# A fused attention and feed-forward layer on one core: the order of each attention turn, and the passage to the feed-forward part

## What is computed

```python
x = x + tanh(g_xattn) * attention_part(layernorm(x), ctx)
x = x + tanh(g_ffn) * ffn_part(layernorm(x))

# attention_part: the first 257 context rows only, so all 128 here
q = rms_norm(x @ q_w.T + q_b) * norm_q_w         # 16 heads of 32
k = rms_norm(ctx @ k_img_w.T + k_img_b) * norm_k_img_w
v = ctx @ v_img_w.T + v_img_b
out = softmax(q k^T / sqrt(32)) v @ o_w.T + o_b

# ffn_part
route = top_k(h @ gate_w, 2)[0].sum(-1)           # h: [tokens, 512]
y = square(relu(h @ up_w)) @ down_w + (h @ expert_weight) * route
y = layernorm(y) * ln_gamma + ln_beta             # up_w: 512 x 2048
```

## Time and profile before

| | |
|---|---|
| Median of 3 runs | 1451.87 us (1451.42 to 1457.24) |
| Profiled execution, its own time | 1454.03 us |
| Its span, first to last instruction | 1452.2 us |
| PE busy | 1364.3 us (94%), 9264 matmuls |
| PE weight loads | 1145.4 us (79%) |
| DVE / ACT / POOL busy | 942.7 (65%) / 595.0 (41%) / 524.4 us (36%) |
| Mean granted TensorE clock | 0.986 of full |

### The profile page before, as it was taken

One profiled execution on the slowest core, in us unless ns is written; L12 is line 12 of the kernel. 1 busy time (PEld: TensorE's weight loads), 2 busy tenths in 40 slices (PEclk: granted clock), 3 DMA queues, 4 the chain that ended last, 5 costly groups with the idle time before them and its releaser, 6 DMA issues.

```text
span 1452.2 us, 28145 instructions
## 1 busy us (share of the span) xinstructions
PE 1364.3 (94%) x9264; PEld 1145.4 (79%) x9264; DVE 942.7 (65%) x1765; ACT 595.0 (41%) x1863; POOL 524.4 (36%) x673
## 2 busy tenths in 40 slices
PE   6799999999999988989999999999999999999996
PEld 4677777777777777779888888789888888888895
DVE  4555555556666656479687577577686785775854
ACT  3666666666666665643231221212312312312120
POOL 2455555555555445664213014013022130140121
PEclk9899999999999999999999999999999999999998
DMA  6123333333332140135754845746738549458540
GB/s 219 51 87 101 97 100 98 100 98 105 102 101 79 59 126 29 37 116 189 194 170 143 239 151 149 222 138 177 228 124 213 185 131 244 145 149 239 169 152 29
DMA packets 215090, 199.15 MB, mean 137 GB/s; under 512 B 126320, under 2 KB 126448, under 8 KB 215024
## 3 DMA queue, kind: packets, MB, share of 16 engines
q1 hardware_dynamic: 214448, 197.26, 45.2%
q10 hardware_dynamic: 576, 1.05, 0.2%
HBM read 156.32 MB, written 41.94 MB: 137 GB/s over the span
## 4 chain that ended last, share of the span: by engine, by line
PE 36%; issue 19%; POOL 17%; DVE 8%; DMA 7%; SPq 6%; ACT 2%; POOLq 0%; DVEq 0%; ACTq 0%
PE bank L75 7%; PE bank L77 7%; PE bank L76 7%; POOL prob L783 6%; SPq L1398 4%; DMA xn_scratch<-fx 4%; PE wide L76 3%; PE wide L75 3%; PE wide L77 3%; POOL eight L770 2%; DMA wo_lo<-ring_scratch 2%; POOL xres L805 2%; PE bank L291 1%; POOL fy L971 1%; PE wide L306 1%
## 5 line engine op out<-in xcount | busy, mean ns | idle before, releaser
L1550 ACT ACTIVATE hT_hi<-c 128x512 fp32r<-128x512 f32 x128 | 79.9, 631 | 403.0 <-PE wide L77 218.7
L625 ACT ACTIVATE prob<-wide,nmx 128x128 f32<-128x128 f32 x512 | 181.9, 402 | 104.1 <-DVE nmx L459 100.9
L1777 POOL TENSOR_TENSOR pair<-pair,beta 128x512 f32<-128x512 f32 x28 | 39.2, 1401 | 463.4 <-DMA pair<-x_scratch 463.4
L76 PE MATMUL wide<-wo_lo,hT_hi 128*128 128x512 f32 x512 | 203.3, 397 | 0.0
L77 PE MATMUL wide<-wo_hi,hT_lo 128*128 128x512 f32 x512 | 201.9, 394 | 0.0
L75 PE MATMUL wide<-wo_hi,hT_hi 128*128 128x512 f32 x512 | 201.6, 394 | 0.0
L783 POOL TENSOR_TENSOR prob<-prob,rr 128x512 f32<-128x512 f32 x128 | 137.9, 1088 | 146.2 <-DVE rr L467 146.2
L1623 DVE TENSOR_TENSOR hT_lo<-c,hT_hi 128x512 fp32r<-128x512 f32 x128 | 99.4, 796 | 77.2 <-ACT hT_hi L1550 77.1
L625 ACT ACTIVATION_READ_ACCUMULATOR prob<-wide,nmx 128x1 f32 x512 | 124.3, 243 | 0.0
L77 PEld LDWEIGHTS wide<-wo_hi,hT_lo 128*128 128x128 f32 x512 | 96.1, 188 | 22.7
L75 PEld LDWEIGHTS wide<-wo_hi,hT_hi 128*128 128x128 f32 x512 | 96.2, 188 | 21.7
(11 more groups left out here) (230 smaller groups left out, 3656.3 us busy)
## 6 DMA issues: line engine op xcount, KB each, us to landing
wo_hi<-ring_scratch SPq DMA_DIRECT2D x156, 256.0 KB, 3.0
wo_lo<-ring_scratch SPq DMA_DIRECT2D x156, 256.0 KB, 3.4
fx<-x_scratch SPq DMA_DIRECT2D x36, 256.0 KB
xin<-in_x SPq DMA_DIRECT2D x32, 256.0 KB, 2.6
cin<-in_ctxT SPq DMA_DIRECT2D x32, 256.0 KB, 2.8
xres<-in_x SPq DMA_DIRECT2D x32, 256.0 KB, 3.9
x_scratch<-x SPq DMA_DIRECT2D x32, 256.0 KB, 3.0
out_x<-fy SPq DMA_DIRECT2D x32, 256.0 KB
```

The costliest lines, as they stand in the source:

```text
L76: eng.matmul(dst, ah, bl, start=False, stop=False)
L625: i = act.activation(prob[par][:, g, h * P:(h + 1) * P], cols(bank[g], h), ACT.Exp, bias=nmx[:, n:n + 1], scale=1.0, accum_out=rs[:, n:n + 1])
L1550: return act.activation(dst, src, ACT.Copy)
L1777: pool.tensor_tensor(res(g, j), res(g, j), ff.beta[:, :], ALU.add).then_inc(ff.po_r, 1)
```

## The change

The names are those of the kernel. PE takes projection Q directly behind K, and projection O behind three probability transposes; the four `values` run together; `turn_x` waits for `residual_sum(o)`. DVE takes reciprocal 0 ahead of kb, qb ahead of kf, and `residual_sum` behind qf. ACT takes the square sum of qb behind `take_probs` 0. POOL takes the inverse root mean square of the keys behind the third division and that of the queries directly behind the fourth, then `residual`, then `lo_ctx`. `load_first` is spread over slots 23 to 27, behind each slot's other transfers; the statistics and normalising of the first group move to slots 24 to 27, its sums to slots 28 to 30 (into four buffers of their own), and the splitting of gate and first up pieces to the end of slot 30. `drain` and the T orders are laid out anew, with half of the last transposes' copies on DVE (`take_probs`), which also makes T banks 4 to 7 and the `up_lo` of the second pieces stand behind `squares`. In the feed-forward part SP issues a ring load between the two pairs of `out_blocks`, and the second one ahead of `in_blocks`.

```diff
 BTP = [bank[n] for n in (4, 5, 6, 4)]
-BTP_LAST = [bank[n] for n in (4, 5, 4, 5)]
-BO_A, BO_S = bank[3], bank[0]
-BPV, BPV_LAST = bank[0], bank[1]
-t_first = [kf, qf, kb, qb]
...
+BO_S = bank[3]
+BPV = bank[0]
+t_first = [sb(ctx, f"tsum{n}", [P, D]) for n in range(4)]
 def has(b):
...
-                sp.wait_ge(st_x2[m], GB // 2 * DMA)
-            ff.load_first(sp)
         if has(a):
             at_least(sp, dv_x2, a - 1, apart=True)
             load(a, 1 - par, t["x"], xres, ld_r)
...
         if ff.has_half(s - 1):
             ff.q_load(sp, s - 1, 1 - par)
+        if is_slot(s, NB - 9):
+            for m in range(2):
+                sp.wait_ge(st_x2[m], GB // 2 * DMA)
+        if isinstance(s, int) and NB - 9 <= s < NB - 4:
+            ff.load_first(sp, s - (NB - 9))
...
     def turn_x(b):
         at_least(pe, dv_qb, b)
+        at_least(pe, dv_x2, b - 3)
         at_least(pe, dv_xn, b + 1)
         turn(xn, BTX, pe_Tx)
...
         if has(n):
             at_least(pe, po_c, n + 1)
             mm3(pe, BK, cT[1 - par], wk, ready=split_weight(n, 0)).then_inc(pe_K, 1)
-        if has(o):
             at_least(pe, dv_xT, n + 1)
-            project_out(o, BO)
-        if has(a):
-            turn_probs(a, 1 - par, 0)
-            turn_probs(a, 1 - par, 1)
-            turn_probs(a, 1 - par, 2)
-        if has(n):
-            at_least(pe, dv_xT, n + 1)
-            at_least(pe, dv_x2, o + 1)
             mm3(pe, BQ, xT, wq, ready=split_weight(n, 1)).then_inc(pe_Q, 1)
         if is_slot(s, 0):
             pe.wait_ge(dv_vb, 1)
             mm3(pe, BV, cT[1 - par], wv).then_inc(pe_V, 1)
         if has(a):
+            turn_probs(a, 1 - par, 0)
+            turn_probs(a, 1 - par, 1)
+            turn_probs(a, 1 - par, 2)
+        if has(o):
+            at_least(pe, dv_qb, n + 1)
+            project_out(o, BO)
+        if has(a):
             turn_probs(a, 1 - par, 3)
-            values(a, 1 - par, 0)
         if is_slot(n, 0):
             keep_clock(BV, 4, D)
         if has(n):
             at_least(pe, dv_kf, n + 1)
-            at_least(pe, ac_pT, a * NG + 3)
+            if has(a):
+                probs_taken(pe, a, 2)
             turn(kf, BTK, pe_Tk)
         if is_slot(n, 0):
             keep_clock(BV, 8, D)
         if has(a):
-            values(a, 1 - par, 1)
-            values(a, 1 - par, 2)
-            values(a, 1 - par, 3)
+            for g in range(NG):
+                values(a, 1 - par, g)
         if has(n + 1) and not is_slot(n, 0):
             turn_x(n + 1)
...
     def drain(s, a, o):
         scores(s)
+        pe.wait_ge(dv_x2, o)
         project_out(o, BO)
-        turn_probs(a, a % 2, 0)
-        turn_probs(a, a % 2, 1)
-        turn_probs(a, a % 2, 2)
+        for g in range(NG):
+            turn_probs(a, a % 2, g)
+        probs_taken(pe, a, 1)
+        ff.turn(pe, 0, t_first)
+        for g in range(NG):
+            values(a, a % 2, g)
+        ff.turn(pe, 1, t_first)
+        ff.turn(pe, 2, t_first)
+        ff.turn(pe, 3, t_first)
         pe.wait_ge(dv_x2, o + 1)
-        ff.turn(pe, 0, t_first)
-        turn_probs(a, a % 2, 3)
-        values(a, a % 2, 0)
-        values(a, a % 2, 1)
-        values(a, a % 2, 2)
-        ff.turn(pe, 1, t_first)
-        values(a, a % 2, 3)
+        project_out(a, BO)
         turn_probs(s, s % 2, 0)
         turn_probs(s, s % 2, 1)
-        ff.turn(pe, 2, t_first)
-        ff.turn(pe, 3, t_first)
-        project_out(a, BO_A)
+        ff.turn(pe, 4, t_first)
         turn_probs(s, s % 2, 2)
+        ff.turn(pe, 5, t_first)
         turn_probs(s, s % 2, 3)
-        ff.turn(pe, 4, t_first)
-        ff.turn(pe, 5, t_first)
-        values(s, s % 2, 0)
-        values(s, s % 2, 1)
+        pe.wait_ge(dv_x2, a + 1)
         ff.turn(pe, 6, t_first)
-        values(s, s % 2, 2)
-        values(s, s % 2, 3)
+        for g in range(NG):
+            values(s, s % 2, g)
         ff.turn(pe, 7, t_first)
         ff.upward(pe, 0, 0)
...
         if has(s):
             for g in range(NG):
                 maxima(s, g)
...
                 dve.wait_ge(cst, 1)
                 dve.wait_ge(ld_bq, DMA)
         if has(s):
-            inverse(s, 0)
             inverse(s, 1)
         if has(n + 1) and has(a):
             normalise(n + 1, par)
         if has(s):
             inverse(s, 2)
-        if has(o):
-            residual_sum(o, par, BO)
+        if has(n) and has(s):
+            at_least(dve, pe_Q, n + 1)
...
             inverse(s, 3)
         if starting:
             stats(1, 1)
-        if has(n):
             at_least(dve, pe_Q, n + 1)
             dve.tensor_tensor(as_strips(qb[:, :]), as_strips(BQ), by_strip(bq[:, :]), ALU.add).then_inc(dv_qb, 1)
...
         if has(n):
             at_least(dve, po_rq, n + 1)
             dve.tensor_scalar(qf[:, :], qb[:, :], rq[:, 0:1], None, ALU.mult).then_inc(dv_qf, 1)
+        if has(o):
+            residual_sum(o, par, BO)
         if starting:
             for k in range(KT // 2, KT):
...
             dve.tensor_scalar(tgbo[:, :], tgbo[:, :], tanh_g[:, 0:1], None, ALU.mult).then_inc(cst, 1)
         if ff_tile(s) is not None:
             ff.stats(dve, 0, ff_tile(s))
+        if is_slot(s, NB - 2):
+            ff.split_gate_lo(dve)
+            for m in range(3):
+                ff.up_lo(dve, 0, m)
...
             maxima(s, g)
         inverse(s, 0)
         residual_sum(o, o % 2, BO)
+        take_probs(a, 1)
         inverse(s, 1)
+        take_probs(a, 3)
+        inverse(s, 2)
         ff.lo_T(dve, 0, 0)
-        inverse(s, 2)
+        split_values(a)
+        ff.lo_T(dve, 0, 1)
         inverse(s, 3)
-        ff.lo_T(dve, 0, 1)
-        ff.up_lo(dve, 0, 0)
-        ff.up_lo(dve, 0, 1)
-        split_values(a)
         ff.lo_T(dve, 0, 2)
+        residual_sum(a, a % 2, BO)
         ff.lo_T(dve, 0, 3)
-        ff.split_gate_lo(dve)
-        residual_sum(a, a % 2, BO_A)
+        take_probs(s, 1)
         ff.lo_T(dve, 0, 4)
+        take_probs(s, 3)
         ff.lo_T(dve, 0, 5)
-        ff.up_lo(dve, 1, 0)
-        ff.up_lo(dve, 1, 1)
         ff.lo_T(dve, 0, 6)
         ff.lo_T(dve, 0, 7)
         ff.sum_2(dve, 0, 0)
         split_values(s)
         ff.sums_all(dve, 0, 0)
         ff.squares(dve, 0, 0)
+        ff.up_lo(dve, 1, 0)
+        ff.up_lo(dve, 1, 1)
         residual_sum(s, s % 2, BO_S)
         ff.prepare(dve)
...
         exps(s, par, 3)
         if has(a):
             take_probs(a, 0)
+        square_q(n)
+        if has(a):
             take_probs(a, 1)
             take_probs(a, 2)
         if has(n + 1):
             hi_ctx(n + 1, par)
         if has(a):
             take_probs(a, 3)
-        square_q(n)
         take_kT(n)
         if has(a):
             hi_aT(a)
...
             ff.q_split_hi(act, s - 2, par)
+        if is_slot(s, NB - 2):
+            ff.split_gate_hi(act)
+            act.wait_ge(pe_K, NB)
+            for m in range(3):
+                ff.up_hi(act, 0, m)
     def drain(s, a, o):
-        act.wait_ge(pe_V, NB)
-        for m in range(3):
-            ff.up_hi(act, 0, m)
         exps(s, s % 2, 0)
         exps(s, s % 2, 1)
         take_probs(a, 0)
-        take_probs(a, 1)
         take_probs(a, 2)
+        exps(s, s % 2, 2)
         ff.hi_T(act, 0, 0)
-        exps(s, s % 2, 2)
-        take_probs(a, 3)
+        hi_aT(a)
+        ff.hi_T(act, 0, 1)
         exps(s, s % 2, 3)
-        ff.hi_T(act, 0, 1)
-        hi_aT(a)
-        take_probs(s, 0)
-        take_probs(s, 1)
         ff.hi_T(act, 0, 2)
         ff.hi_T(act, 0, 3)
-        ff.split_gate_hi(act)
-        for m in range(2):
-            ff.up_hi(act, 1, m)
+        take_probs(s, 0)
+        ff.hi_T(act, 0, 4)
         take_probs(s, 2)
-        take_probs(s, 3)
-        ff.hi_T(act, 0, 4)
         ff.hi_T(act, 0, 5)
         ff.hi_T(act, 0, 6)
         ff.hi_T(act, 0, 7)
+        ff.copy_1(act, 0, 0)
         hi_aT(s)
-        ff.copy_1(act, 0, 0)
         ff.copy_5(act, 0, 0)
-        ff.up_hi(act, 1, 2)
+        for m in range(3):
+            ff.up_hi(act, 1, m)
     run(act, slot, before, drain)
...
         if is_slot(s, 0):
             inv_rms_k(n)
         divide(s, par, 1)
+        divide(s, par, 2)
         if not is_slot(s, 0):
             inv_rms_k(n)
-        divide(s, par, 2)
         divide(s, par, 3)
+        inv_rms_q(n)
+        if has(a):
+            residual(a, 1 - par)
         if has(n + 1):
             lo_ctx(n + 1, par)
-        if has(a):
-            residual(a, 1 - par)
-        inv_rms_q(n)
+        if is_slot(s, NB - 4):
+            ff.up_sums(pool, 0)
+        if is_slot(s, NB - 3):
+            ff.x_sums(pool, 0, 0, t_first)
         if is_slot(s, NB - 2):
-            ff.up_sums(pool, 0)
+            ff.x_sums(pool, 0, 1, t_first)
         if has(s + 3):
             inv_std(s + 3)
         if ff_tile(s) is not None:
...
     def drain(s, a, o):
         divide(s, s % 2, 0)
         divide(s, s % 2, 1)
-        ff.up_lo(pool, 0, 2)
```

(41 more changed lines are left out.)

58 lines of the change are left out of this document (34 added, 24 removed).

## The result

The changed kernel took 1420.84 us (median of 4 runs, 1419.5 to 1421.94) beside 1453.84 us for the kernel before (4 runs): a ratio of 0.9771 [0.9745, 0.9797]. It is 33 us faster; 1418 us was forecast. The profiled executions differ by 33.9 us: 1420.12 against 1454.03 us.

What follows compares the result with a forecast made beforehand. PE plus four kinds of stops bound the kernel; 14.3 + 7.6 + 3 + 1.3 + 4.2 + 4 = 34.4 us off 1454.03 gives 1419.6, the run median 2.2 lower, so 1418 us; range 1390 to 1437.

Steps and rivals of the forecast that it cites:

- The steady slot: Slots 2 to 26 and 29: `residual` holds qf, the wait moves to `turn_x`; 0.55 us gained per slot, 14.3 us together.
- The sign of being wrong: Prediction wrong if the steady period does not change, or spread loads make xres late in slots 23 to 27.
- one xres load that has 10 us to spare: Spread loads: the largest burst, four tiles (1 MB), stands ahead of one xres load not needed for 10 us.
- Slots 27 and 28: Spreading the load burst gains 6.5 us of stop and half clock, plus 2 x 0.55: 7.6 us (3 to 7.6).
- The start: Slots 0 and 1: rq comes sooner before slot 1's qf turn, half clock may go; 3 us (1 to 5).
- the fourth transpose covers the delay of the copies: Steady slot: ACT's earlier square sum delays a pT copy by about 0.8 us, which the fourth transpose covers.
- The passage: Scores of 31 to second quarter of up: 6.5 us less a PE wait of 2.5 to 3; net 4.2 (0 to 7).
- The feed-forward part: Weight loads waited 9.7 us for the ring; ring loads issued sooner gain 4 us (-2 to 11).
- PE becomes the bound: Rival, chance 0.20: `residual` does not hold up qf, 28 slots gain about 1.0 us more: 1390 us.
- the wait only moves: Rival, chance 0.14: qb late for O, or kf longer than 0.75 us, eats the 0.55 per slot: 1433 us.
- The rival through the clock: Rival, chance 0.06: `residual_sum` held beside `lo_ctx`, PE waits 2.3 us at `turn_x`, half clock follows: about 1495 us.
- no change: Rival, chance 0.05: `residual_sum` held but no clock loss; 28 x 0.6 = 17 us lost, less 20 gained.

Runs made afterwards that it cites:

- all three edits together: Changed kernel with POOL waiting for qf before `residual`, `residual_sum` ahead of qf, and the second pieces' `up_lo` ahead of `squares`: 1388.8 us, ratio 0.9556.
- the first experiment: Changed kernel with POOL made to wait for qf before it starts `residual`: 1395.34 us, ratio 0.9599 to the kernel before.
- the experiment: Changed kernel with all first feed-forward loads back in slot 27 and the statistics in slots 27 to 30: 1427.72 us, ratio 0.9814.
- The old order put back: Changed kernel with SP's feed-forward order of ring loads and block transfers as in the kernel before: 1424.19 us, ratio 0.9791.
- the two kernels in which the hold is taken away: Changed kernel with POOL waiting for qf before `residual`, 1395.34 us; changed kernel with `residual_sum` ahead of qf on DVE, 1389.66 us.

## Why the prediction was right, and where it was not

**The steady slot** was right in mechanism, link by link: kf 0.75 us forecast and measured, qf 1.50 us for the forecast 1.51 (321.14 to 322.65), the residual sum unstretched, the wait moved to `turn_x` and released by L478 (now L485), Q ahead of O at no cost. The 0.55 us was right as a mean only, and neither kind of slot has it.

The forecast was made on a loop slot of 18.30 us, and the slot shown above is its counterpart: it gained 0.26 us. Counted from the scores, its reciprocal 2, kf, qf and residual sum all came within 0.1 us of the forecast. What was too small is the end: the turn of xn started 0.24 us behind the sum, not 0.05, and the turn of qf 0.49 us behind that, not 0.41. In a written-out slot the first of these is 0.10 us, and the chain itself is 0.35 us earlier (rk 8.02 instead of 8.37 us behind the scores), so PE waits 0.93 instead of 1.44 us. Two things are different in the chain. One is seen only in every second loop slot, those of 18.05 us: DVE's normalising of xn starts 0.08 us ahead of division 1 on POOL there (0.16 us elsewhere) and takes 1.41 us, and the reciprocal behind it, for which division 2 and then rk wait, comes later. In a written-out slot it takes 0.54 us:

```profile
359.24 0.54 DVE L456 TENSOR_SCALAR xn<-xin,mv,rstd 128x512 f32<-128x512 f32 x1
...
402.96 0.63 PE L302 MATMUL bank<-ident,xn 128*128 128x128 f32 x4 [0.93 <-issue]
```

But it takes 0.54 us in the other loop slots too, and those are still 0.27 us longer than written-out ones. The other, in both kinds of loop slots, is a later start of the exponentials (2.15 and 2.29 instead of 2.03 us behind the scores); to it comes the 0.24 us between the sum's end and PE. Why the loop has the last two is open, and no run here separates them.

**The sign of being wrong.** The prediction called itself wrong if the spread loads made xres late in slots 23 to 27. They did, in slot 24. The step that failed is "one xres load that has 10 us to spare":

```profile
459.50 2.97 SPq L220 DMA_DIRECT2D xres<-in_x  x1
...
470.76 0.49 DVE L559 TENSOR_SCALAR qf<-qb,rq 128x512 f32<-128x512 f32 x1 [2.06 <-POOL rq L775]
471.16 0.75 DVE L485 SCALAR_TENSOR_TENSOR x<-bank,tanh_g,xres 128x512 f32<-128x512 f32 x1
...
472.29 1.28 POOL L819 TENSOR_TENSOR xres<-xres,tgbo 128x512 f32<-128x512 f32 x1 [1.57 <-DMA xres<-in_x]
```

Behind the four tiles of slot 23 the issue alone took 2.97 us, and POOL waited 1.57 us for xres, 12.8 us behind the start of its issue. It cost PE nothing, and slot 24 even took only 16.54 us, with no wait at all: `residual` could not start beside qf, which therefore took 0.49 us. That the total did not suffer is luck, not the margin of 10 us; with all three edits together the same late load cost 1.2 us. The trace of the changed kernel thus held the first experiment in itself, once. Without this accident slots 2 to 26 and 29 would have gained 13.4 us, not 14.4.

**Slots 27 and 28** gained 8.0 for 7.6 forecast. The spread loads give 8 us in the kernel before as well, so this term stands by itself. But within the new order a burst costs by another route, as the experiment showed: not through qf, but through `lo_ctx` and the next K.

**The start** gained 3.7 us for 3, of which 2.9 in slots 0 and 1, but not by the way forecast. In slot 1 the wait of 2.60 us before qf's turn did go. In its place PE waited for copies of pT on ACT:

```profile
59.57 0.66 PE L340 MATMUL bank<-ident,prob 128*128 128x128 f32 x4 [2.77 <-ACT pT L621]
61.25 1.08 PE L302 MATMUL bank<-ident,kf 128*128 128x128 f32 x4 [1.02 <-ACT pT L621]
```

The waits of slot 1 fell only from 4.6 to 3.8 us, and the lower clock, which "may go", stayed (0.82 and 0.84 in the mean of the slot). The step that failed is that the fourth transpose covers the delay of the copies: in slot 1 there is no output projection in front of it. That the size came out is luck.

**Slot 30** gained 1.6 for 1.3.

**The passage** seems to have gained 4.3 for 4.2. The stop before the second quarter's first product was 2.31 us where 2.5 to 3 was forecast, released by the subtraction named. But the 4.2 was to include the clock's part of the stop, and this lies behind the line that the table draws: before, the second quarter takes 2.97 us to the gate's small matmuls, after 4.56, at the lower clock. Up to there the passage gained 2.7 us, not 4.2. The term was too large by this clock part, 1.6 us. The other waits there were 0.55 us for a pT copy and 0.86 us for the low part:

```profile
585.79 0.65 PE L340 MATMUL bank<-ident,prob 128*128 128x128 f32 x4 [0.55 <-ACT pT L621]
...
597.61 0.63 PE L1049 MATMUL bank<-ident,fx 128*128 128x128 f32 x4 [0.86 <-DVE wv_lo L1134]
```

**The feed-forward part** then was nearer than the table says. From the gate's small matmuls to the end it gained 3.4 us (806.9 to 803.5) for the 4 forecast, and the ring waits fell by 3.1 us, from 9.7 to 5.4 + 1.2 = 6.6 us. The old order put back confirms the size. Still, the 4 was taken from bounds of -2 to 11, with no row that said how much sooner a ring tile would land: it was a guess that came out.

So 33.9 us measured for a sum of 34.4 hides two errors of opposite sign, the accident of slot 24 (1.0 more) and the clock part of the passage (1.6 less), and one term, the start, whose size was luck. The steady slots, the burst and slot 30, 24 of the 34 us, were right in size and, with the reservations above, in mechanism.

**The rivals.** That PE becomes the bound was said to give 1390 us if `residual` did not hold qf; the changed kernel is not that case, but the two kernels in which the hold is taken away measured 1395.34 and 1389.66 us. The price of that rival, 1.0 us in 28 slots, was right: both kinds of slot lost 1.0 us when the hold went. The Trainium skill (SBUF — State Buffer, "Who interferes with whom") was weighed there: its rule on which VectorE instructions GpSimd excludes is borne out by 1.50 us for qf beside `residual` and 0.49 without it, by 0.75 us for kf with POOL idle and 1.52 beside a division, and by 0.74 us for the sum that reads PSUM beside `lo_ctx`. That the wait only moves (1433) did not happen: PE waits nowhere for qb in these slots, and kf is 0.75 us. The rival through the clock did not happen either, since the residual sum is not held and PE's waits from 100 to 500 us stay at 1.6 us or less. For the same reason "no change" fell. That such a clock loss exists is shown by the kernel with inv_rms_q last: waits of some 3 us in each slot, where the rival had 2.3, gave 1534.55 us, more than the 1495 of that rival. What kf's fall from 1.52 to 0.75 us is worth by itself was not tested.
